# Layer 2's routing stage: weights and head constants loaded from another point, constant rows by DMA from stored patterns, VectorE's additions between pieces of other jobs

## The chip, the core and the metric

One core of one Trainium2 chip runs the whole program. The metric is the device time of one execution in microseconds (us). The kernel before took 1200.81 us, the median of 3 runs (1198.93 to 1203.05).

## What is computed

Two layers on x of 4 x 512 tokens of width 256. Each layer is x + attention(LN(x)) + FFN(LN(x)), cut here to what matters:

```python
xn = _layernorm(x)                    # layer 1: selective scan + mixture of 16 experts, 4 a token
x = x + _L0_attn_ref(xn, ...) + _L0_ffn_ref(xn, ...)
xn = _layernorm(x)                    # layer 2: chunked scan (SSD) with 64 heads + 16 experts, 2 a token
x = x + _L1_attn_ref(xn, ...) + _L1_ffn_ref(xn, ...)
# _L1_ffn_ref: scores = sigmoid(xn @ gate_w.T); top 2, normalised; dw = their weights
#   y = mlp(xn, sw1, sw2, sw3) + sum over experts of mlp(xn, w1[e], w2[e], w3[e]) * dw[:, e]
# _L1_attn_ref: dt = softplus(proj + bias); A = -exp(A_log); c = cumsum(dt * A) in each chunk
#   Lmat = exp(c[t] - c[s]) for s <= t; states and outputs from Lmat, then gate, norm, projection
```

## The kernel before

Five instruction streams (TensorE `pe`, ScalarE `act`, VectorE `v`, GpSimd `pool`, SyncE `sp`) run in program order and meet at semaphores; the order in each is written out by hand. Layer 1 fills the first half of the execution. Then, for layer 2:

- **Scan out and layer norm.** SP reloads the sums in 8 DMAs of 512 KB (`sums0_load`, L1204), two for each batch of four row tiles. TensorE adds them to the scan's rows (`scan_out_tensor`, L1215 and L1217; tile t = 4b waits for batch b), VectorE adds to x. GpSimd's last accumulating DMA of layer 1 is L1156. After the layer norm TensorE transposes the rows into `xnT` (L226), and SP stores them to `xn_d` (L232).
- **Routing stage** (`phase1_tensor`, `phase1_scalar`, `phase1_vector`). It interleaves three jobs. (1) The shared expert: 12 "up" products n = 0 to 11 (`shared_up_tensor`, L686: eight matmul records, gate then up), each followed by a tanh on ScalarE (L707) and two operations on VectorE (`shared_silu`, L714 and L716); after n = 4, 7, 10 and at the end, four "down" products (`shared_down_tensor`, L698), each added to x by VectorE (`shared_add`, L726). Up product n waits for silu n-2, down product t for addition t-2, since each pair has two banks. (2) Routing: logits (L283), a copy out and transposition back (L320, L292, L327), scores (L335), sigmoid (L342, L344), maxima (L347), their indices (L353, cast in L357), mask (`route_mask_vector`), ranks on TensorE (L299), counts and slots, one-hot rows (L428, L436, L445), token numbers on TensorE (L307) and indices for the gathers (`route_index_vector`, L457 to L460). (3) The scan's step sizes: `dt_tensor` (L1573), `dt_first_scalar`, `dt_log_vector` (L1610 to L1615), `dt_sum_vector` (L1623 to L1630), `dt_parts_vector` (L1637 to L1641), `dt_weights_vector` (L1646). In the VectorE stream `dt_log_vector`, `dt_sum_vector` and `dt_parts_vector` each stand whole ahead of a group of four additions.
- **GpSimd beside it** (`load1_pool`): the shared weights' DMAs (L2284 to L2289), issued once the first row of the layer norm is there, then `dt_weights_pool` and `scan1_constants`: memsets and `affine_select`s over `seg_l` (94 x 1024, bf16) and `crow` (88 x 4096, bf16) (L1507 to L1520). Later it gathers rows for the experts (L1491).
- **SP beside it**: `head_weights` (L1542, L1545) once the first row of the layer norm is there, `layernorm_sync`, `scan1_weights` (L1551 to L1557), `combine_store`, then `heads_out_sync`: three DMAs `cp_d` of the cumulative sums' parts (L1762) when semaphore `dt_dve` has reached `CP_READY`, eight DMAs `dec_d` (L1766), and a wait for all of them (`HEADS_STORED`); behind it `scan1_sync`, with the constants, the first chunk's rows and the weights of the first three experts (L1480, L1481).
- **Scan stage** (`scan1_*`). TensorE starts with `dw_tensor` (L1728, L1734) once all 16 additions are done, then the projections (L1846), the first expert's products (L1417, L1430) between them. ScalarE (L1960) and VectorE wait for `HEADS_STORED` before their first instruction of this stage. TensorE takes expert 0's gate and up product between projections 2 and 3.

Three lines set up waits that the steps touch:

```python
CP_READY order: DT_SUM, CP_READY, DT_W, W_READY = 1, 2, 3, 4   # counts of dt_dve
sp.wait_ge(dt_dve, CP_READY)                                   # heads_out_sync, L1760
act.wait_ge(heads_stored, HEADS_STORED)                        # scan1_scalar
```

Of the kernel before, what the change touches and what calls it, by code (L numbers as in the profile page):

```python
# [28 lines left out]
E = 16  # L29
# [54 lines left out]
def _program(nc, a, out, ctx):  # L84
# [6 lines left out]

    bank = ctx.enter_context(nc.psum_tensor("bank", [P, 8, 512], F32))
# [21 lines left out]
    yo = sb("yo", [P, 5, D])  # L114

# [206 lines left out]
    def route_scores_vector(v, l, nr, m):  # L322
# [6 lines left out]
        if l == 0:  # L329
            vec.done(nc.vector.tensor_reduce(m["mx"], logits[:, :, 0:E], X, ALU.max))  # L330
            v.wait_ge(vec.sem, vec.now)
            nc.vector.tensor_tensor(score, logits[:, :, 0:E], m["mx"].unsqueeze(2).to_broadcast([P, TT, E]),
                                    ALU.subtract).then_inc(s.score_in, 1)
        else:
            nc.vector.tensor_copy(score, logits[:, :, 0:E]).then_inc(s.score_in, 1)  # L335
# [13 lines left out]
    def route_pick_vector(v, l, K, m):  # L349
        top, top_i = m["top"], m["top_i"]  # L350
        v.wait_ge(vec.sem, vec.now)
        for t in range(TT):
            vec.done(nc.vector.max_index(top_i[:, t, :], top[:, t, :], m["score"][:, t, :]))  # L353
# [378 lines left out]
    with ExitStack() as c0:  # L732
# [352 lines left out]
        def layer0_scalar(act):  # L1085
# [9 lines left out]
            act.wait_ge(delta_ready, 4)  # L1095
            gate_tanh(act, 0)
# [137 lines left out]
    HEADS, HD, NS, C1, Q = 64, 8, 128, 768, 64  # L1234
# [7 lines left out]
    with ExitStack() as c1a, ExitStack() as c1:  # L1242
# [76 lines left out]
        w_heads = sem("w_heads")  # L1319

        dt_pe, dt_act, dt_dve = sem("dt_pe"), sem("dt_act"), sem("dt_dve")
        DT_TAKEN, DT_LOG, DT_E, DT_EXP = 2, 3, 4, 5
        DT_SUM, CP_READY, DT_W, W_READY = 1, 2, 3, 4
# [179 lines left out]

        def scan1_constants(pool):
            sel = seg_l[:, :, :, :].rearrange("p s g (h t) -> p (s g) h t", t=Q)
            rows = slice(Q, SEG)
            poo.done(nc.gpsimd.memset(seg_l[:, :, :, :], 0.0))  # L1507
            poo.done(nc.gpsimd.memset(crow[0:Q + 24, :, :, :], 0.0))
            poo.done(nc.gpsimd.memset(xpad[:, :, 0:3], 0.0))
            poo.done(nc.gpsimd.memset(xq[:, :, :, :, :, :], 0.0))  # L1510
            pool.wait_ge(poo.sem, poo.now)
            poo.done(nc.gpsimd.affine_select(out=crow[0:Q, :, :, :], in_=crow[0:Q, :, :, :], compare_op=ALU.is_ge, fill=NEVER,
                                             base=0, pattern=[[0, 2 * HP], [1, Q]], channel_multiplier=-1))
# [34 lines left out]
        def scan1_weights(sp):  # L1548
# [4 lines left out]
            for to, src in ((w_in[:, :, :], a["w_in1"].rearrange("(k p) n -> p k n", p=P)),  # L1553
# [3 lines left out]
                sp.dma_start(to, src).then_inc(w_ssd, 16)  # L1557

        UPS1 = NB * F1
        RANKS1_UP, TOKENS1_UP = 4, 10  # L1560

        def downs1_at(n):

# [84 lines left out]
        def phase1_tensor(pe):  # L1648
# [3 lines left out]
            for n in range(UPS1):  # L1652
# [7 lines left out]
                if n == TOKENS1_UP:  # L1660
                    route_tokens_tensor(pe, 1, K1, m1)
# [747 lines left out]
```

## Time and profile before

| | |
|---|---|
| median of 3 runs | 1200.81 us (1198.93 to 1203.05) |
| profiled execution | 1205.48 us, its span 1203.7 us |
| mean granted TensorE clock | 0.935 |
| busy: TensorE, VectorE, ScalarE, GpSimd | 976.7, 914.1, 497.0, 434.9 us |
| routing stage, from the logits to the last addition | about 604 to 711 us of the span |

Times in the rows are counted from the span's start. A row of the timeline is one group of instructions that ran behind one another; what stands in brackets is how long the engine had been idle and what released it. PE is TensorE, DVE VectorE, ACT ScalarE, POOL GpSimd, SPq SyncE's DMA issues. The granted clock is 1.00 at 2.4 GHz and 0.50 at 1.2 GHz.

### The profile page before, as it was taken

How to read it: one execution, taken by the hardware profiler on the slowest of the kernel's cores; microseconds unless marked ns; L12 is line 12 of the kernel's file. 1: busy time of each engine (PE TensorE's matmuls, PEld its weight loads, DVE VectorE, ACT ScalarE, POOL GpSimd, SP SyncE). 2: the span in 40 equal slices, each digit the busy share in tenths (PEclk: the TensorE clock that was granted, in tenths of full speed). 3: DMA queues.
4: the chain of work that ended last, by engine and by line, in shares of the span. 5: the costliest groups of instructions: out<-in, count | busy, mean ns of one | idle time of the engine just before them, and what ended most of it. 6: DMA issues, size and time to landing. Idle time of an engine off the chain costs nothing. (4 is left out here: it accounts for less than half of the span.)

```text
span 1203.7 us, 18601 instructions
## 1 busy us (share of the span) xinstructions
PE 976.7 (81%) x6048; PEld 578.1 (48%) x6048; DVE 914.1 (76%) x1506; ACT 497.0 (41%) x1130; POOL 434.9 (36%) x332
## 2 busy tenths in 40 slices
PE   3987997788787778773787686889988988899885
PEld 2354555444444444441634353445555555456553
DVE  4659567989999999999657746677677767677676
ACT  2201135554555555543121124545455554554542
POOL 0000100777787877753171010322322232133310
PEclk9989999989999999995798798999998999999998
DMA  6960172787878878878650041443433343244524
GB/s 220 369 172 1 52 164 74 134 155 144 165 148 156 162 149 159 147 141 182 142 148 5 0 99 38 112 95 86 112 87 93 87 106 93 67 95 104 116 40 141
DMA packets 107092, 143.27 MB, mean 119 GB/s; under 512 B 30022, under 2 KB 97334, under 8 KB 102710
## 3 DMA queue, kind: packets, MB, share of 16 engines
q0 software_dynamic: 30368, 77.92, 33.5%
q1 hardware_dynamic: 76630, 64.14, 19.2%
q8 instruction: 52, 0.85, 0.3%
q14 instruction: 42, 0.34, 0.1%
HBM read 72.80 MB, written 39.46 MB: 93 GB/s over the span
## 5 line engine op out<-in xcount | busy, mean ns | idle before, releaser
L1501 POOL DMA_INDIRECT sum<-yo,to_i x48 | 78.0, 1624 | 317.1 <-ACT yo L1459 301.2
L1171 POOL DMA_INDIRECT xg<-xn_d,token_i x80 | 96.2, 1203 | 175.1 <-DVE to_i L460 93.4
L1164 POOL DMA_INDIRECT sum<-yo,to_i x80 | 140.3, 1754 | 46.8 <-DMA sum<-yo,to_i 23.7
L1011 PE MATMUL bank<-areaA,xgT 128*128 x320 | 120.6, 502 | 15.0 <-issue 9.9
L1028 PE MATMUL bank<-areaA,hidT 88*128 x320 | 91.7, 410 | 45.8 <-ACT hidT L1076 41.7
L2048 DVE TENSOR_TENSOR areaD<-areaD,gb 128x512 f32<-128x512 f32 x128 | 87.5, 688 | 53.0 <-ACT areaD L1995 49.2
L1028 PEld LDWEIGHTS bank<-areaA,hidT 88*128 88x128 f32 x320 | 55.6, 193 | 76.7 <-issue 72.1
L686 PE MATMUL bank<-xnT,areaB 128*128 128x512 f32 x192 | 86.8, 599 | 0.8 <-DVE y L716 0.8
L1846 PE MATMUL bank<-xnT,w_in 128*128 128x512 f32 x160 | 85.5, 661 | 2.2 <-ACT ecn L1751 1.5
L1011 PEld LDWEIGHTS bank<-areaA,xgT 128*128 128x128 f32 x320 | 56.8, 196 | 58.0 <-issue 41.5
L1491 POOL DMA_INDIRECT xg<-xn_d,token_i x48 | 53.9, 1123 | 82.6 <-DVE to_i L460 68.2
L1995 ACT ACTIVATE areaD<-bank 128x512 f32<-128x512 f32 x128 | 75.9, 593 | 17.0 <-PE bank L1838 15.8
L1058 ACT ACTIVATE areaB<-delta,a_neg 128x1022 f32<-128x1022 f32 x64 | 72.8, 1137 | 4.2 <-DVE areaB L1145 4.2
L1430 PE MATMUL bank<-wst,xgT 128*128 128x352 f32 x192 | 71.3, 496 | 3.6 <-ACT xgT L1446 3.5
L707 ACT ACTIVATE areaB<-bank 128x512 f32<-128x512 f32 x24 | 14.3, 597 | 122.0 <-PE bank L686 122.0
L1083 ACT ACTIVATE yo<-bank,slot_w 128x256 f32<-128x256 f32 x80 | 37.7, 472 | 59.3 <-PE bank L1028 53.5
L2103 DVE SCALAR_TENSOR_TENSOR cv<-xpad,conv_w,cv 128x512 f32<-128x512 f32 x72 | 54.1, 751 | 8.4 <-ACT cv L1961 6.7
L981 PE MATMUL bank<-parts,pick 96*128 96x512 bf16 x128 | 40.6, 400 | 22.7 <-DVE xnT L1145 11.9
L686 PEld LDWEIGHTS bank<-xnT,areaB 128*128 128x128 f32 x192 | 35.4, 190 | 48.4 <-issue 44.4
L1885 PE MATMUL bank<-areaD,xq 128*32 128x64 f32 x2048 | 56.2, 231 | 2.9 <-DVE areaD L2056 2.9
L698 PE MATMUL bank<-areaB,y 128*128 128x256 f32 x192 | 48.3, 413 | 11.2 <-DVE x L728 11.2
L1885 PEld LDWEIGHTS bank<-areaD,xq 128*32 128x32 f32 x2048 | 35.7, 112 | 44.7 <-issue 34.8
(342 smaller groups left out, 2141.6 us busy)
## 6 DMA issues: line engine op xcount, KB each, us to landing
y<-xnT POOLq DMA_DIRECT2D x21, 1024.0 KB
wst<-gu_f SPq DMA_DIRECT2D x96, 176.0 KB
y<-areaB POOLq DMA_DIRECT2D x11, 1024.0 KB
wst<-down_f SPq DMA_DIRECT2D x48, 176.0 KB
areaA<-in_gu SPq DMA_DIRECT2D x2, 2816.0 KB
gu_f<-in_gu POOLq DMA_DIRECT2D x1, 5632.0 KB, 17.0
sum<-yo SPq DMA_DIRECT2D x2, 2176.0 KB, 16.2
down_f<-in_down POOLq DMA_DIRECT2D x1, 2816.0 KB, 22.6
```

Of the source, the lines that this page charges most:

```text
L686: last = nc.tensor.matmul(bank[:, b, :], w[:, k, f * P:(f + 1) * P], xnT[:, k, c * 512:(c + 1) * 512], start=(k == 0), stop=(k == KD - 1))
L1011: last = nc.tensor.matmul(bank[:, GB + q % 2, 0:2 * FI], xgT[:, q % 2, k, :], wgu0_of(e, k), start=(k == 0), stop=(k == KD - 1))
L1028: last = nc.tensor.matmul(bank[:, HY, 0:D], hidT[:, q % 2, h, :], wd0_of(e, h), start=(h == 0), stop=(h == 1))
L1058: nc.scalar.activation(dA[:, u % 2, :].rearrange("p (b t) -> p b t", b=2)[:, :, 1:L], view[:, :, 1:L], ACT.Exp, scale=a_neg[:, hf, n:n + 1 ...
L1164: nc.gpsimd.indirect_dma_start(sum0_d[q % 2], bass.IndirectOffsetOnAxis(ap=to_i[:, q:q + 1], axis=0), yo[:, q % 5, :], None, compute_op=AL ...
L1171: nc.gpsimd.indirect_dma_start(xg[:, q % 5, :], None, xn_d[0], bass.IndirectOffsetOnAxis(ap=token_i[:, q:q + 1], axis=0)).then_inc(s.gathe ...
L1430: last = nc.tensor.matmul(bank[:, eb, 0:2 * FI], xgT[:, q % 2, k, :], wgu_of(q, k), start=(k == 0), stop=(k == KD - 1))
L1501: nc.gpsimd.indirect_dma_start(sum1_d, bass.IndirectOffsetOnAxis(ap=to_i[:, q:q + 1], axis=0), yo[:, q % 4, :], None, compute_op=ALU.add). ...
L1846: last = nc.tensor.matmul(o, w_in[:, k, col:col + P], xnT[:, k, b * L:(b + 1) * L], start=(k == 0), stop=(k == KD - 1))
L1885: last = nc.tensor.matmul(bank[32 * c:32 * c + 32, YB, at_t:at_t + Q], window, mm[:, g, j * Q:(j + 1) * Q], start=(old % 2 == 0 and g == 0 ...
L1995: nc.scalar.activation(ex[:, g % 2, :], o, ACT.Exp).then_inc(free, 1)
L2048: nc.vector.tensor_tensor(mm[:, g, :].rearrange("p (j t) -> p j t", t=Q), ex[:, g % 2, :].rearrange("p (j t) -> p j t", t=Q), gb[:, step % ...
```

## The change

The order of the streams changes in the routing stage, some work moves to the program's start, and the layer-2 constants come by DMA:

- `patterns_pool` builds one 94 x 640 bf16 tile at the program's start; `patterns_store` writes it to HBM (SP, behind the clearing of the sums). `crow_pattern_sync` and `seg_pattern_sync` fill `crow` (704 rows of 1 KB) and `seg_l` (752 rows of 256 B) from it with broadcast reads. The affine_selects over the full tiles go; the memsets of `xpad`, `xq` and `restart` move ahead.
- `load1_pool` waits for the end of layer 1's scan (`hc_ready`) in place of the first row of the layer norm, and `head_weights` for the end of layer 1's experts.
- The scores are copied from PSUM directly (`route_scores1_vector`; the second copy, L335, goes); four of the sixteen `max_index` move one step forward.
- `dt_log_vector`, `dt_sum_vector` and `dt_parts_vector` are cut into pieces, one for each addition of a group; `route_slots_vector` moves from n = 6 to n = 8; the one-hot rows, `dt_weights_vector`, the token rows, the index and the parts move back, so that `CP_READY` is reached at the stage's end. TensorE's token product moves behind down product 12.

```diff
@@ route_scores1_vector (new), route_find_vector (new, cut out of route_pick_vector)
+    def route_scores1_vector(v, m):
...
+        nc.vector.tensor_copy(m["score"].rearrange("p (c j) n -> p c j n", j=4), by_token[:, :, :, 0:E]).then_inc(s.logits, 1)
+        v.wait_ge(s.logits, LOGITS_READ)
+        v.sem_inc(s.score_in, 1)
@@ layer0_scalar
             act.wait_ge(delta_ready, 4)
+            act.wait_ge(pattern_stored, 16)
@@ order of dt_dve
-        DT_SUM, CP_READY, DT_W, W_READY = 1, 2, 3, 4
+        DT_SUM, DT_W, CP_READY, W_READY = 1, 2, 3, 4
@@ patterns
+        def patterns_pool(pool):
...
+            poo.done(nc.gpsimd.memset(pat, 0.0))
...
+            pool.sem_inc(patterns, 1)
+        def patterns_store(sp):
+            sp.wait_ge(patterns, 1)
+            sp.dma_start(pat_d, pat).then_inc(pattern_stored, 16)
+        def crow_pattern_sync(sp):
+            sp.wait_ge(pattern_stored, 16)
+            sp.wait_ge(ly[0].y_ready, NT0)
+            sp.dma_start(crow[0:Q + 24, :, :, :].rearrange("p s (g j) t -> p (s g) (j t)", j=8),
+                         pat_d[0:Q + 24, P:].unsqueeze(1).to_broadcast([Q + 24, 2 * G1, 8 * Q])).then_inc(pattern_rows, 16)
+        def seg_pattern_sync(sp):
+            sp.wait_ge(q1.xn_rows, TT)
+            sp.dma_start(seg_l[:, :, :, :].rearrange("p s g x -> p (s g) x"),
+                         pat_d[:, 0:P].unsqueeze(1).to_broadcast([SEG, 2 * G1, P])).then_inc(pattern_rows, 16)
         def scan1_constants(pool):
+            pool.wait_ge(ly[0].y_ready, NT0)
             poo.done(nc.gpsimd.memset(xpad[:, :, 0:3], 0.0))
             poo.done(nc.gpsimd.memset(xq[:, :, :, :, :, :], 0.0))
+            pool.wait_ge(q1.xn_rows, 1)
             poo.done(nc.gpsimd.memset(restart[:, :], 1.0))
...
         def head_weights(sp):
-            sp.wait_ge(q1.xn_rows, 1)
+            sp.wait_ge(ly[0].y_ready, NT0)
         def scan1_weights(sp):
+            seg_pattern_sync(sp)
@@ phase1_tensor
-                if n == TOKENS1_UP:
-                    route_tokens_tensor(pe, 1, K1, m1)
...
                 shared_down_tensor(pe, 1, F1, sd1, shT1, NB - 1, j)
+                if j == 0:
+                    route_tokens_tensor(pe, 1, K1, m1)
@@ phase1_vector
+                if n == 4:
+                    for j in range(4):
+                        dt_log_vector(v, j)
+                        shared_add(v, 1, None, 0, j)
...
+                if n == 7:
+                    for j in range(4):
+                        dt_sum_vector(v, j)
+                        shared_add(v, 1, None, 1, j)
+                if n == 8:
                     route_slots_vector(v, 1, K1, m1)
                 if n == 9:
+                    route_rows_vector(v, 1, K1, m1, 0, 2 * part)
+                    dt_weights_vector(v)
                 if n == 10:
                     for j in range(4):
+                        if j < 2:
+                            route_rows_vector(v, 1, K1, m1, (2 + j) * part, (3 + j) * part)
+                        else:
+                            route_tile_rows_vector(v, 1, K1, m1, (j - 2) * 2 * part, (j - 1) * 2 * part)
+                        shared_add(v, 1, None, 2, j)
+            route_token_rows_vector(v, 1, K1, m1, 0, TT)
             for j in range(4):
                 shared_add(v, 1, None, NB - 1, j)
+                if j == 1:
+                    route_index_vector(v, 1, m1)
+                dt_parts_vector(v, j)
@@ scan1_sync: the wait for the constants
-            sp.wait_ge(consts1, 2)
+            sp.wait_ge(pattern_rows, 16 * 2)
@@ load1_pool
-            pool.wait_ge(q1.xn_rows, 1)
+            pool.wait_ge(hc_ready, UN)
@@ the streams
             clear_sums(sp)
+            patterns_store(sp)
...
             head_weights(sp)
+            crow_pattern_sync(sp)
             layernorm_sync(sp, 1, xn_tok1)
...
             constants(pool)
+            patterns_pool(pool)
```

## Rows read from the trace of the kernel before

**Rows 1.** Windows: engines' busy us (instructions), granted TensorE clock, DMA share, GB/s.

```profile
660.00:680.00 20.00, 11.82 (x30) 7.08 (x29) 11.36 (x24) 2.32 (x3) 0.00 (x0) 0.74 0.00 0
...
800.00:1100.00 300.00, 273.80 (x2587) 163.51 (x2576) 216.18 (x425) 151.52 (x359) 86.38 (x63) 0.97 0.39 91
```

**Rows 2.** Waits, 600 to 712 us: us in total, times, longest.

```profile
PE bank L698 <- DVE x L726: 8.9, 3, 8.2
```

**Rows 3.** Timeline of VectorE, five short operations of the same engine.

```profile
616.85 2.59 DVE L335 COPY area<-area 128x256 f32<-128x256 f32 x1
...
620.67 4.06 DVE L342 TENSOR_SCALAR area<-area 128x256 f32<-128x256 f32 x1
...
631.80 3.55 DVE L357 CAST area<-area 128x32 f32<-128x32 uint32 x1
...
661.88 0.18 DVE L416 CAST area<-area 128x32 int32<-128x32 f32 x1
...
711.56 1.13 DVE L2018 TENSOR_SCALAR w_out<-w_out,norm_w 128x256 f32<-128x256 f32 x4
```

**Rows 4.** Timeline of GpSimd beside them.

```profile
615.23 4.07 POOL L1512 TENSOR_SCALAR_AFFINE_SELECT crow<-crow 64x4096 bf16<-64x4096 bf16 x1 [0.15 <-POOL xq L1510]
...
620.51 4.08 POOL L1518 TENSOR_SCALAR_AFFINE_SELECT crow<-crow 24x4096 bf16<-24x4096 bf16 x1
```

**Rows 5.** Timeline of TensorE in the routing stage and after it.

```profile
608.94 3.67 PE L686 MATMUL bank<-xnT,sg 128*128 128x512 f32 x4 [3.40 <-DMA sd<-in_sdown]
...
668.85 1.65 PE L698 MATMUL bank<-sd,area 128*128 128x256 f32 x3 [8.18 <-DVE x L726]
...
698.17 1.88 PE L686 MATMUL bank<-xnT,sg 128*128 128x512 f32 x4
...
703.90 7.13 PE L698 MATMUL bank<-sd,area 128*128 128x256 f32 x24 [2.13 <-DVE area L716]
711.55 1.97 PE L1728 MATMUL bank<-ident,areaD 128*128 128x128 f32 x16 [0.52 <-DVE x L726]
...
721.35 1.35 PE L1430 MATMUL bank<-wst,xgT 128*128 128x352 f32 x4
```

**Rows 6.** Timeline of VectorE: a job ahead of additions, and the last addition.

```profile
640.00 1.22 DVE L1610 SCALAR_TENSOR_TENSOR areaD<-areaD 128x1024 f32<-128x1024 f32 x1
...
644.45 0.74 DVE L726 TENSOR_TENSOR x<-bank,x 128x256 f32<-128x256 f32 x2
...
651.88 0.69 DVE L714 SCALAR_TENSOR_TENSOR th<-th,bank 128x512 f32<-128x512 f32 x1 [3.64 <-ACT th L707]
...
663.89 0.87 DVE L1623 TENSOR_SCALAR areaD<-areaD,a 128x512 f32<-128x512 f32 x2
...
679.63 4.42 DVE L428 TENSOR_TENSOR area<-area,iota 128x4096 f16<-128x4096 f32 x1
...
711.07 0.42 DVE L726 TENSOR_TENSOR x<-bank,x 128x256 f32<-128x256 f32 x1 [0.87 <-PE bank L698]
```

**Rows 7.** Timeline of SyncE's DMA issues at the stage's end.

```profile
695.17 1.75 SPq L1762 DMA_DIRECT2D cp_d<-areaD  x3
696.97 5.19 SPq L1766 DMA_DIRECT2D dec_d<-areaD  x8
711.59 0.34 SPq L1776 DMA_DIRECT2D dec<-dec_d  x1
...
715.42 0.94 SPq L1480 DMA_DIRECT2D wst<-gu_f  x2
```

**Rows 8.** Timeline of ScalarE, its first instruction of the scan's loop.

```profile
717.97 0.60 ACT L1960 ACTIVATE xpad<-bank 128x512 f32<-128x512 f32 x1 [2.22 <-PE bank L1846]
```

**Rows 9.** Timeline of TensorE: row tile 12 of the scan out.

```profile
586.20 0.60 PE L1215 MATMUL bank<-areaA,ident 128*128 128x256 f32 x2
```

**Rows 10.** DMA queues, 580 to 585 us (first) and 605 to 610 us: packets, MB, share.

```profile
q1 hardware_dynamic: 1185, 1.16, 66.2%
...
q0 software_dynamic: 319, 0.32, 30.5%
```

More of the change, by code:

```diff
@@ L347, in route_top_vector, with route_find_vector, route_pick_vector @@
             vec.done(nc.vector.max(m["top"][:, t, :], score[:, t, :]))
-    def route_pick_vector(v, l, K, m):
+    def route_find_vector(v, m, t0, t1):
+        v.wait_ge(vec.sem, vec.now)
+        for t in range(t0, t1):
+            vec.done(nc.vector.max_index(m["top_i"][:, t, :], m["top"][:, t, :], m["score"][:, t, :]))
+    def route_pick_vector(v, l, K, m, t0=0):
         top, top_i = m["top"], m["top_i"]
-        v.wait_ge(vec.sem, vec.now)
-        for t in range(TT):
-            vec.done(nc.vector.max_index(top_i[:, t, :], top[:, t, :], m["score"][:, t, :]))
+        route_find_vector(v, m, t0, TT)
         vec.done(nc.vector.tensor_reduce(m["mx"], top[:, :, 0:K], X, ALU.add))
@@ L1517, in scan1_constants @@
-            for part in range(3):
-                poo.done(nc.gpsimd.affine_select(out=by_group, in_=by_group, compare_op=ALU.not_equal, fill=-1.0,
-                                                 base=-part * 8, pattern=[[0, 2 * G1], [-1, 8], [0, Q]], channel_multiplier=1))
-                poo.done(nc.gpsimd.affine_select(out=sel[rows], in_=sel[rows], compare_op=ALU.not_equal, fill=1.0,
-                                                 base=-(24 + 2 * part), pattern=[[0, 2 * G1], [-1, 2], [0, Q]], channel_multiplier=1))
-                pool.wait_ge(poo.sem, poo.now)
@@ L1531, in dt_weights_pool @@
+            pool.sem_inc(consts1, 2)
+        def dt_weights_pool(pool):
             pool.wait_ge(heads_in, 16 * 5)
@@ L1559, in _program @@
         UPS1 = NB * F1
-        RANKS1_UP, TOKENS1_UP = 4, 10
+        RANKS1_UP = 4
         def downs1_at(n):
@@ new lines, in dt_sum_vector @@
+        def dt_sum_vector(v, j):
+            v.wait_ge(vec.sem, vec.now)
+            if j == 0:
+                v.wait_ge(a_ready, 2)
+                for hf in range(2):
+                    vec.done(nc.vector.tensor_scalar(hk(rest1)[:, hf], dtT[:, hf], a1[:, hf:hf + 1], None, ALU.mult))
+            if j in (1, 2):
+                v.wait_ge(consts1, 1)
+                vec.done(nc.vector.tensor_tensor_scan(cT[:, j - 1, :], restart[:, :], rest1[:, j - 1, :], 0.0, ALU.mult, ALU.add))
+            if j == 3:
+                for hf in range(2):
+                    by_chunk = hk(cT)[:, hf]
+                    last = nc.vector.tensor_tensor(l1[:, hf, :, :], by_chunk[:, :, Q - 1:Q].to_broadcast([P, CH, Q]), by_chunk, ALU.subtract)
+                last.then_inc(dt_dve, 1)
@@ L1684, in phase1_vector @@
             route_rows_of_logits_vector(v, 1, m1)
+            part = n1 // 4
             for n in range(UPS1):
```

122 lines of the change are left out of this document (56 added, 66 removed).

## The prediction

> **What bounds the kernel now.** I read the windows first. In the scan stage behind, TensorE is busy 273.8 of 300 us; in the routing stage it has 11.8 of 20 us in one window, at a mean granted clock of 0.74 [rows 1]. The change touches the routing stage, so the question is what holds TensorE there. The waits say: VectorE's additions, 8.9 us in three waits [rows 2]. The timeline shows the pattern. A whole job of VectorE stands ahead of four additions (640.00 to 644.45, then the additions), down products 2 and 3 can't start, and then VectorE waits 3.64 us for up product 5 [rows 6]. The longest such hole on TensorE is 8.18 us, and the work behind it is slow [rows 5]. Second, three short operations of VectorE take 2.59, 4.06 and 3.55 us, where one like the second takes 0.28 (1.13 for four) and a cast of the same size as the third 0.18 [rows 3]. Each ends about when a 4.1 us affine_select of GpSimd over `crow` does: the first at 619.4 with the one that began at 615.23; there are four of these [rows 4]. Third, up product 0 waits 3.40 us for its weights, and its first half takes 3.67 us instead of 1.88 [rows 5]. The stage ends for TensorE with the last addition, 711.07 + 0.42 = 711.5 [rows 6].
>
> **The change, part by part.** I walked the three streams in order, each instruction starting when its engine is free and what it waits for is there: up product 3.43 us (two halves 1.72 apart, 1.88 the last shown) [rows 5], silu 1.33, addition 0.37, down product 1.28 us, everything at 2.4 GHz. The old order gives the last addition at 706.0, where the trace has 711.5; the 5.5 us are spells at 1.2 GHz, as behind the 8.18 us hole. The new order, walked in the same way, gives 687.4, so **18.6 us less** at full clock:
> - Weights earlier: -5.0. The wait (3.4) goes, and with it the slow first half (3.67 - 1.88 = 1.8, less 0.2 of overlap) [rows 5].
> - GpSimd's full tiles go: L335 goes (2.5), L342 becomes 0.3 (-3.8), L357 0.2 (-3.4), 9.7 in all [rows 3]. VectorE then waits 3.7 us for the tanhs (an up product and a `dt` product take 5.3 us a step), so -6.0.
> - dt_log in pieces: -0.3 only. The first addition comes 1.2 us behind silu 4 instead of 4.45, but silu 4 itself is now late: `dt_first_scalar` holds ScalarE for 5.8 us, which VectorE's slowness hid before.
> - Slots moved, dt_sum in pieces: -6.2. Between silu 6 and the first addition stood 2.4 + 2.9 + 1.3 + 4.5 = 11.1 us, now 2.4 + 1.3 + 0.95 = 4.7. The job begins at 663.89 before [rows 6].
> - Rows and parts: -5.0. From silu 8's end to the first addition were 4.3 [rows 6] + 1.3 + 3.8 + 1.3 + 4.6 = 15.3 us, now 2.9 + 1.3 + 3.4 + 1.3 + 1.1 = 10.0; the pieces give 0.3 back.
> - The tail: +4.0. Token rows (1.9), TensorE's token product (1.35) and the parts' pieces now lie between up product 11 and the last addition.
>
> Clock: the new walk leaves TensorE three idle stretches of 2 to 3 us and one of 1.8. In the trace a stretch of 2.13 us is followed by products that take 7.13 us for 24 records, where 12 take 2.57 at full clock [rows 5], so one such stretch costs about 2 us. Bounds 0 and 8; I take 4, against 5.5 before, so **-1.5**. The Trainium skill speaks against the change here: "TensorE: Matmul & The Clock Gate", section "HAM oscillation", tells of kernels whose short idle gaps send the clock back and forth, each burst starting cold. By that every gap would pay, which I estimate at 8 to 10 us instead of 4 and a total of 1195 instead of 1190.
>
> Transfers: the shared weights (1.1 MB) are now issued at about 571 instead of 595, behind L1156 on GpSimd's queue, while SP's last reloads still run: 1185 packets, 66.2% of 16 engines over 5 us, so 45 ns each [rows 10]. The weights were 960 packets, at 75 ns where nothing held them (319 in 30.5%) [rows 10]. On one engine of 16 the two together need 74 x 0.045 + 60 x 0.075 = 7.8 us instead of 3.3, so the last reload lands 4.5 us later, at about 588.4 instead of 583.9. Row tile 12 wants it at 586.20 [rows 9]: **+2.2** on everything behind. Bounds: 0 (the reload is served first) and 4.5 (no slack at tile 12).
>
> Costed at nothing: the patterns at the start (GpSimd is idle there, SP issues one DMA more ahead of a load with 100 us to spare); the broadcasts into `crow` and `seg_l` on SP (first read in the scan stage; w_heads behind them has some 3 us); `head_weights` on SP earlier; the memsets on GpSimd; the stored rows of the layer norm, which silu 0 waits for and which land about when the first tanh is ready (5 us later costs 0.7 in the walk); the gathers, whose index comes 4 us ahead of the last addition and which TensorE wants 6 us behind it. If the first cover fails the price is under 1 us each.
>
> The export: `CP_READY` moves from 16 us ahead of the last addition (695.17) to 0.7 us behind it. Behind the wait on SP are queued three DMAs (1.8 us of issue), eight DMAs (5.19), their landing, then the constants and the experts' weights [rows 7]. Counting from the last addition: issue ends at 0.75 + 1.8 + 5.2 = 7.75, landed at about 9.4 (1.7 us for a small DMA: no row shows it; at least 1, and 4 if they collide with the gathers). ScalarE, which began its loop at 717.97 - 711.49 = 6.5 [rows 8], is held to 9.4: +2.9. The first expert's weights are issued at 9.4 + (715.42 - 711.59) = 13.2 instead of 3.9 [rows 7] and land some 4 us later, at 17.3, while TensorE took the product at 721.35 - 711.49 = 9.9 [rows 5]: +7.4 for it, and project 3 stands behind it in TensorE's order, at half clock after a 4.7 us hole. ScalarE had some slack on project 3, so the scan begins later by between 2.9 and 9.3; nearest the product's own +7.4, I take **+7.0**. TensorE bounds what follows [rows 1], so none of it comes back.
>
> Sum: -18.6 - 1.5 + 2.2 + 7.0 = **-10.9 us**. The profiled execution took 1205.5 (span 1203.7 + 1.8), 4.7 above the median of the runs; against the median the forecast is 1200.8 - 10.9 = **1190 us**.
>
> **Rivals.**
> 1. *The export costs little.* If ScalarE's slack hides the late weights and only +2.9 is left, the time is 1186; with a clock that stays up, 1182. For it: ScalarE and VectorE, not TensorE, set the pace of the first projections. Chance 0.17.
> 2. *The gain stays, but SP gives it back.* cp_d and dec_d share engines with four gathers that are in flight then; if they land 4 us late and the reload costs 4.5, 1190 + 4 + 2.3 = 1196 to 1199, nearly no change. Chance 0.10.
> 3. *Slower: TensorE's clock.* Place: from down product 2 to the last addition, some 54 us. The pieces cut one long hole into many short ones. If the clock is granted in full in none of them, each 3.4 us at half clock costs 1.7. The gain is gone and the kernel slower by 0.3% from (10.9 + 3.6) / 1.7 = 8.5 such spells beyond the two or three I count, 11 in all, or 38 of the 54 us; fully half clock gives about 1213. For it: a mean of 0.74 in a window of before. Against it: that window had the 8.18 us hole. The Trainium skill's section on oscillation, cited above, is the rule that would bring it about. Chance 0.05.
> 4. *The change doesn't do what it says:* the three slow operations aren't GpSimd's doing. Then about 6 us stay in, and the time is 1196. Against it: all three end with an affine_select [rows 3, 4]. Chance 0.03.
>
> **How the numbers follow.** The forecast has 0.65. Its own bounds (clock -4 to +4, transfers -2.2 to +2.3, export -4.1 to +2.3, partly together) give 1183 to 1197; with most of rivals 1 and 2 the range is 1181 to 1198. About 0.3%, 3.6 us, is what a measurement of this kernel can tell from no change. Faster by more needs a time below 1197.2: all of the forecast but a little, rivals 1 and 4: 0.87. Within 0.3%: most of rival 2 and the forecast's rim, 0.08. Slower: 0.05.
>
> **What would show it.** Right: L342 near 0.3 us, the last addition at 691 to 696, TensorE's waits for additions under 3 us each, row tile 12 waiting 1 to 3 us for a reload, cp_d issued behind the last addition, ScalarE idle to 9 us behind it, the first expert product 15 us or more behind it. Wrong: a last addition later than 700, or a scan stage that starts as soon behind it as before.

## The result, and the profile after

The changed kernel took 1195.82 us (median, 1189.17 to 1200.18 in 14 runs), the kernel before 1202.86 (1198.41 to 1208.05 in 14 runs beside it): **ratio 0.9935, 95% interval 0.9914 to 0.9957**, so 7.8 us less by the ratio (5.2 to 10.3; the two medians differ by 7.0). The forecast was 1190 us and 10.9 us less; the range 1181 to 1198 holds the result. Of the 5.8 us between forecast and result, 2.1 are the kernel before, whose median was 1200.81 in the 3 runs that the forecast started from.

The profiled execution took 1190.80 us, its span is 1189.0, the clock 0.945. Against the span of before it is 14.7 us shorter, more than the runs say. The reason lies upstream: layer 1's scan out began at 568.70 instead of 572.97 us, though of layer 1's streams only ScalarE's has something new in it, one wait for the stored patterns; in the profiles of this study it began anywhere from 568.7 to 576.1. So I compare stretches, each from a fixed event to the next, and not spans.

TensorE's timeline of the changed kernel: row tile 12 of the scan out, the logits and up product 0, the products that wait for an addition, the scan's first transposes, and the first expert product:

```profile
568.70 1.19 PE L1229 MATMUL bank<-areaA,ident 128*128 128x256 f32 x2 [10.95 <-DMA y<-areaB]
...
584.54 0.67 PE L1229 MATMUL bank<-areaA,ident 128*128 128x256 f32 x2 [2.92 <-DMA x<-sum]
...
601.98 1.92 PE L288 MATMUL bank<-xnT,wr 128*32 128x512 f32 x16 [0.74 <-ACT xnT L219]
603.83 1.98 PE L699 MATMUL bank<-xnT,sg 128*128 128x512 f32 x4
...
632.28 2.86 PE L711 MATMUL bank<-sd,area 128*128 128x256 f32 x12 [2.33 <-DVE x L739]
...
649.46 3.01 PE L711 MATMUL bank<-sd,area 128*128 128x256 f32 x12 [1.43 <-DVE x L739]
...
668.40 4.54 PE L711 MATMUL bank<-sd,area 128*128 128x256 f32 x12 [3.04 <-DVE x L739]
...
688.53 3.19 PE L1784 MATMUL bank<-ident,areaD 128*128 128x128 f32 x16 [2.13 <-DVE x L739]
...
709.69 2.71 PE L1446 MATMUL bank<-wst,xgT 128*128 128x352 f32 x4 [2.35 <-DMA wst<-down_f]
```

Against [rows 5]: up product 0 has no wait for weights and a fast first half, and the 8.18 us hole is now at most 3.04 us. Row tile 12, which had no wait [rows 9], now waits 2.92 us for the reload. Twelve down records take 2.86 and 3.01 us behind waits of 2.33 and 1.43, and 4.54 behind the wait of 3.04.

VectorE's timeline, what answers to [rows 3] and [rows 6]:

```profile
613.39 0.29 DVE L352 TENSOR_SCALAR area<-area 128x256 f32<-128x256 f32 x1
...
620.99 0.12 DVE L370 CAST area<-area 128x32 f32<-128x32 uint32 x1
...
629.35 0.69 DVE L727 SCALAR_TENSOR_TENSOR th<-th,bank 128x512 f32<-128x512 f32 x1 [2.78 <-ACT th L720]
...
688.06 0.42 DVE L739 TENSOR_TENSOR x<-bank,x 128x256 f32<-128x256 f32 x1
```

The operations of 4.06 and 3.55 us take 0.29 and 0.12; silu 4 waits for the tanh; the last addition ends at 688.5 instead of 711.5. What happened behind it stands in SyncE's DMA issues and in one row of ScalarE:

```profile
689.15 2.49 SPq L1818 DMA_DIRECT2D cp_d<-areaD  x3
691.68 4.67 SPq L1822 DMA_DIRECT2D dec_d<-areaD  x8
702.08 0.35 SPq L1832 DMA_DIRECT2D dec<-dec_d  x1
...
705.54 0.94 SPq L1496 DMA_DIRECT2D wst<-gu_f  x2
```

```profile
702.24 0.60 ACT L2016 ACTIVATE xpad<-bank 128x512 f32<-128x512 f32 x1 [8.16 <-DMA dec_d<-areaD]
```

Against [rows 7, 8]: the last `dec_d` is issued at 696.35, and the wait for it ends at 702.05. ScalarE begins its loop 13.8 us behind the last addition (6.5 before), the first expert product comes 21.2 us behind it (9.9 before).

### The profile page after: what moved, and what is told of

Its sections match the earlier page's. It is cut to its first block, busy times and chain, and to the rows that moved or that the text cites. A ratio compares the mean times of both kernels' runs of the same rounds, so it can differ in the third digit from the quotient of the medians.

```text
span 1189.0 us, 18608 instructions
## 1 busy us (share of the span) xinstructions
PE 970.0 (82%) x6048; PEld 573.3 (48%) x6048; DVE 902.7 (76%) x1508; ACT 495.4 (42%) x1130; POOL 413.9 (35%) x331
## 3 DMA queue, kind: packets, MB, share of 16 engines
q0 software_dynamic: 30368, 77.92, 33.1%
## 4 chain that ended last, share of the span: by engine, by line
PE 45%; DVE 22%; DMA 10%; issue 8%; ACT 6%; POOL 6%; SPq 2%; ACTq 1%; DVEq 0%; POOLq 0%
PE bank L699 7%; DMA sum<-yo,to_i 6%; PE bank L1902 6%; PE bank L1446 4%; PE bank L711 4%; POOL sum L1178 3%; PE bank L1452 3%; POOL xg L1185 3%; DVE cv L2159 2%; PE bank L1941 2%; PE bank L1024 2%; DVE xnT L1159 2%; PE bank L1885 2%; PE bank L1041 2%; PE bank L1894 2%
## 5 line engine op out<-in xcount | busy, mean ns | idle before, releaser
L1185 POOL DMA_INDIRECT xg<-xn_d,token_i x80 | 95.9, 1198 | 175.7 <-DVE to_i L473 94.0
L1024 PE MATMUL bank<-areaA,xgT 128*128 x320 | 116.2, 486 | 15.6 <-issue 8.7
L1902 PE MATMUL bank<-xnT,w_in 128*128 128x512 f32 x160 | 86.7, 668 | 6.6 <-ACT cv L2017 5.4
L1041 PEld LDWEIGHTS bank<-areaA,hidT 88*128 88x128 f32 x320 | 54.9, 190 | 76.4 <-issue 72.1
L1507 POOL DMA_INDIRECT xg<-xn_d,token_i x48 | 54.4, 1133 | 104.4 <-DVE to_i L473 90.0
L2051 ACT ACTIVATE areaD<-bank 128x512 f32<-128x512 f32 x128 | 75.8, 592 | 16.1 <-PE bank L1894 14.7
L994 PE MATMUL bank<-parts,pick 96*128 96x512 bf16 x128 | 40.6, 400 | 22.4 <-DVE xnT L1159 11.0
L711 PE MATMUL bank<-areaB,y 128*128 128x256 f32 x192 | 48.8, 416 | 11.2 <-DVE x L741 11.2
## 6 DMA issues: line engine op xcount, KB each, us to landing
gu_f<-in_gu POOLq DMA_DIRECT2D x1, 5632.0 KB, 18.5
```

What stands on the lines that cost most here:

```text
L711: last = nc.tensor.matmul(bank[:, 4 + n % 2, 0:D], shT[:, (c * F + f) % shT.shape[1], j * P:(j + 1) * P], sd[:, f, :], start=(f == 0), sto ...
L1024: last = nc.tensor.matmul(bank[:, GB + q % 2, 0:2 * FI], xgT[:, q % 2, k, :], wgu0_of(e, k), start=(k == 0), stop=(k == KD - 1))
L1041: last = nc.tensor.matmul(bank[:, HY, 0:D], hidT[:, q % 2, h, :], wd0_of(e, h), start=(h == 0), stop=(h == 1))
L1185: nc.gpsimd.indirect_dma_start(xg[:, q % 5, :], None, xn_d[0], bass.IndirectOffsetOnAxis(ap=token_i[:, q:q + 1], axis=0)).then_inc(s.gathe ...
L1902: last = nc.tensor.matmul(o, w_in[:, k, col:col + P], xnT[:, k, b * L:(b + 1) * L], start=(k == 0), stop=(k == KD - 1))
```

## The experiments

The table has the same stretches from each of the fourteen profiles, in us. Scan out: from its first row tile to the logits. Then, counted from the logits: the start of silu 4, and the ends of the four groups of additions A to D (D is the last addition). Silu 4 is VectorE's first operation on up product 4. Last two columns: from D to ScalarE's loop and to the first expert product.

| kernel | ratio (95%) | scan out | silu 4 | A | B | C | D | ScalarE | expert |
|---|---|---|---|---|---|---|---|---|---|
| before | 1 | 30.7 | 35.1 | 44.6 | 71.1 | 95.2 | 107.9 | 6.5 | 9.9 |
| after | 0.9935 (0.9914-0.9957) | 33.3 | 27.4 | 34.2 | 51.9 | 71.4 | 86.5 | 13.8 | 21.2 |
| e1 export first | 0.9899 (0.9858-0.9940) | 33.3 | 27.4 | 34.2 | 51.9 | 71.5 | 86.6 | 7.9 | 14.7 |
| e2 weights wait | 0.9912 (0.9881-0.9944) | 29.6 | 27.4 | 35.1 | 53.6 | 73.2 | 88.3 | 15.0 | 22.6 |
| e3 experts early | 0.9837 (0.9805-0.9870) | 32.6 | 27.4 | 34.9 | 53.6 | 73.0 | 88.4 | 7.2 | 10.6 |
| e4 both | 0.9844 (0.9806-0.9881) | 31.2 | 27.4 | 34.2 | 51.9 | 71.5 | 86.5 | 7.6 | 11.0 |
| e5 patterns alone | 1.0036 (1.0005-1.0068) | 30.3 | 38.5 | 49.8 | 76.4 | 100.5 | 113.2 | 6.5 | 9.9 |
| e6 orders alone | 1.0000 (0.9972-1.0028) | 30.0 | 36.5 | 45.6 | 63.4 | 83.0 | 98.1 | 14.2 | 22.4 |
| e7 affines back | 0.9850 (0.9805-0.9894) | 32.7 | 27.4 | 34.2 | 51.9 | 72.4 | 86.7 | 7.2 | 10.4 |
| e8 jobs whole | 0.9992 (0.9960-1.0024) | 34.9 | 27.4 | 39.6 | 63.3 | 87.9 | 102.9 | 7.6 | 10.9 |
| e9 weights alone | 1.0144 (1.0106-1.0182) | 56.6 | 29.6 | 40.7 | 67.0 | 91.1 | 103.8 | 6.5 | 9.9 |
| e10 patterns, weights | 0.9982 (0.9949-1.0016) | 35.5 | 27.4 | 39.6 | 65.3 | 89.4 | 100.4 | 6.5 | 9.9 |
| e11 additions first | 0.9756 (0.9720-0.9792) | 30.2 | 27.4 | 33.0 | 49.7 | 67.5 | 82.0 | 7.3 | 10.7 |
| e12 two first | 0.9765 (0.9725-0.9805) | 31.0 | 27.4 | 33.1 | 49.7 | 68.2 | 83.3 | 7.8 | 11.2 |

### The export and the reload: e1 to e4

**e1**: the changed kernel with the eight `dec_d` DMAs, whose data is long there, ahead of the wait for `CP_READY`.

```diff
+            sp.wait_ge(dt_act, DT_E)
+            for b in range(NB):
...
             sp.wait_ge(dt_dve, CP_READY)
             for r in range(3):
...
-            sp.wait_ge(dt_act, DT_E)
-            for b in range(NB):
...
```

> The changed kernel, with the eight small dec_d DMAs issued ahead of the three cp_d DMAs instead of behind them (they need only ScalarE's exponentials, which are there some 30 us before the last addition). Theory A (the changed kernel loses 7 to 10 us behind its stage because ScalarE waits for dec_d's landing, 13.8 us behind the last addition where it was 6.5 before, and the experts' weights are issued behind that): ScalarE's loop begins 6 to 8 us behind the last addition, the first expert product 14 to 16 us behind it instead of 21.2, and the time falls by 5 to 7 us below the changed kernel, to a ratio of about 0.988 of the kernel before. Rival (the landing is late for the gathers and cp_d that share the DMA engines, so it is cp_d that will be late now): ScalarE still begins 11 us or more behind the last addition, gain under 2 us.

Everything up to D is as in the changed kernel, and ScalarE's loop comes 7.9 us behind D instead of 13.8, released by TensorE and no longer by a DMA:

```profile
699.16 0.60 ACT L2016 ACTIVATE xpad<-bank 128x512 f32<-128x512 f32 x1 [2.22 <-PE bank L1902]
```

The expert product stays late (14.7): its weights are still queued behind `HEADS_STORED`. The profile gives 6 us or more; the ratio by itself (0.9899 against 0.9935, each against its own runs of before) doesn't tell e1 from the changed kernel.

**e2**: the changed kernel, but GpSimd issues the shared weights once the last reload has landed (`pool.wait_ge(x_back[NB - 1], 32)`).

> The changed kernel, with GpSimd waiting for the last reload of layer 1's sums before it issues the shared weights. Theory A (the weights delay the last reload, so that row tile 12 waits 2.9 us): row tile 12 waits for nothing, the stretch from the first row tile to the logits takes 30.6 us as before instead of 33.3, and the weights, issued at about 584, are still there when the logits are done, so 2 to 3 us less than the changed kernel. Rival (the weights, now issued beside the scattered 4-byte loads of the head constants, land after the logits, as in the kernel before): up product 0 waits 1 to 5 us, gain nil or a loss of up to 2 us.

The scan out takes 29.6 us instead of 33.3 and row tile 12 has no wait, so the weights' DMAs are what delayed the reload. In this profile groups A and B come 0.9 and 1.7 us later: the twelve products behind the same wait of 2.33 us took 4.33 us where the changed kernel's took 2.86. So only half of the gain is left at D, and the ratio can't be told from that of the changed kernel. The profiles of the other kernels agree on the cause: with the weights issued at layer 1's end the scan out took 32.6 to 35.5 us (after, e1, e3, e7, e8, e10), with the weights behind the reloads or where they were before, 29.6 to 31.2 (before, e2, e4, e5, e6, e11, e12).

**e3**: as e1, and the weights of the first experts are issued on SP before `cp_d` too.

```diff
+            sp.wait_ge(dt_dve, DT_W)
+            for m in range(-5, 0):
+                expert_sync(sp, m)
             sp.wait_ge(dt_dve, CP_READY)
@@ scan1_sync
-            for m in range(-5, 0):
-                expert_sync(sp, m)
```

> Export first, and also the weights of experts tiles 0 and 1 issued ahead of cp_d, once the expert numbers are there (about 25 us before the last addition). Theory A (behind the export the first expert product still waits for its own weights, and project 3 behind it): the first expert product is taken 9 to 11 us behind the last addition as in the kernel before, TensorE waits for no weights, and 2 to 5 us come off e1's time; ratio to the kernel before 0.983 to 0.988. Rival (VectorE and ScalarE pace the first projections, so that the product is not missed): the time is that of e1 within 1 us.

The first expert product is 10.6 us behind D, near the 9.9 of before, and has no wait for weights. Ratio to before 0.9837 against 0.9935, and the intervals don't meet: the two parts of the export's loss were `dec_d` and the weights behind it.

**e4**: e2 and e3 together.

> e2 and e3 together. If the two losses are separate, as theory A has it, the gains add: 9 to 14 us less than the changed kernel, 17 to 21 less than the kernel before, ratio 0.983 to 0.986. If either turns into a wait elsewhere, it gives no more than the better of the two.

Scan out 31.2, expert product 11.0. The ratio is in the range that I expected but can't be told from e3's, so the runs don't show that the two gains add.

### Where the stage's gain comes from: e5, e6, e9, e10

**e5**: the kernel before with the patterns alone: `patterns_pool`, `patterns_store`, `crow_pattern_sync`, `seg_pattern_sync` and the new `scan1_constants`; waits, weights and orders as before.

> The kernel before with the patterns by DMA and nothing else: the full-tile affine_selects of GpSimd go, the weights, the orders and the second copy of the scores stay. My theory (GpSimd's affine_selects hold VectorE's short operations): the copy, the TENSOR_SCALAR and the cast that took 2.59, 4.06 and 3.55 us take about 0.4, 0.3 and 0.2; the part from the logits to the last addition (107.5 us before) comes to 98 to 102, the export costs nothing (last addition to first product of the scan's experts near 10 us), and the time is 0.4 to 0.8% below before. Rival (they are slow of themselves or by DMA traffic): one or more of the three still takes over 2 us and the ratio is within 0.3% of 1.

Slower, and both theories missed. The three short operations are quick (0.29, 0.28, 0.12 us), as my theory had it, but the stage is 5.3 us longer. TensorE's waits and VectorE's timeline of e5 say why:

```profile
PE bank L702 <- DMA sd<-in_sdown: 8.4, 1, 8.4
```

```profile
621.31 0.69 DVE L730 SCALAR_TENSOR_TENSOR th<-th,bank 128x512 f32<-128x512 f32 x1 [14.78 <-DMA xn_d<-area]
```

```profile
598.45 0.42 SPq L1551 DMA_DIRECT2D crow<-pat_d  x1
601.99 0.38 SPq L237 DMA_DIRECT2D xn_d<-area  x1
602.41 12.71 SPq L1557 DMA_DIRECT2D seg_l<-pat_d  x1
```

The 704 KB broadcast into `crow` goes out 3 us after the first shared weights and just ahead of the layer norm's rows. (`seg_l`'s goes out right behind those rows; the two broadcasts weren't tried apart.) The weights land late (a wait of 8.4 us, 3.4 before), and the rows, which silu 0 waits for, take 19.3 us to land instead of 13.6 (8.5 in the changed kernel, where the broadcast goes out at 577.28).

**e6**: the kernel before with the new orders and pieces alone; affine_selects, late weights and the second copy stay.

> The kernel before with the new order and pieces of VectorE's and TensorE's jobs alone: the affine_selects, the late weights and the second copy stay. My theory: the short operations stay at 2.6 to 4 us, the part from the logits to the last addition is 7 to 12 us shorter than before's 107.5, and nearly all of it is given back behind the last addition, where the first expert product comes about 21 us behind it instead of 10.3: a ratio of 0.997 to 1.003. Rival (the export's loss was that of the weights and not of the order): first expert product within 12 us of the last addition and a ratio under 0.995.

As my theory had it: D comes 9.8 us sooner, the expert product 12.5 us later behind it, and the ratio is 1.0000. ScalarE's row shows the same late landing as in the changed kernel: the last `dec_d` was issued by 708.31, and ScalarE started 6.3 us later.

```profile
714.64 0.60 ACT L1978 ACTIVATE xpad<-bank 128x512 f32<-128x512 f32 x1 [8.58 <-DMA dec_d<-areaD]
```

**e9**: the kernel before with the weights and head constants issued sooner alone (and GpSimd's memset of `restart` held until the layer norm's first row).

```diff
-            pool.wait_ge(q1.xn_rows, 1)
+            pool.wait_ge(hc_ready, UN)
@@ head_weights
-            sp.wait_ge(q1.xn_rows, 1)
+            sp.wait_ge(ly[0].y_ready, NT0)
```

> The kernel before with the shared weights and the head constants issued sooner, and nothing else (GpSimd waits for the layer norm's first row only ahead of its memset of restart). My theory, from the walk's term: up product 0 no longer waits for its weights (3.4 us before) and its first half takes 2 us, so the part from the logits to the last addition comes to 101 to 104 us instead of 107.9; the scan out is 2 to 3 us longer, as in the changed kernel (30.65 to 33.3). Ratio 0.995 to 0.999. Rival (the stage is held by VectorE's short operations behind GpSimd anyway): the stage stays within 1.5 us of 107.9 and the ratio is 1.000 to 1.003.

From the logits to D the number is the one that my theory gave (103.8, 4.0 less than before), but the run doesn't price the weights alone. The full tiles were through before the logits, so the short operations were quick here too:

```profile
640.35 0.28 DVE L342 TENSOR_SCALAR area<-area 128x256 f32<-128x256 f32 x1
...
648.52 0.12 DVE L357 CAST area<-area 128x32 f32<-128x32 uint32 x1
```

And the kernel is 17 us slower by the ratio: the scan out takes 56.6 us instead of 30.7. GpSimd's stream is in order: before, it waited 8.9 us for the head constants and began the full tiles at 609.3; with those constants early the wait is gone, and the full tiles begin at 596.0, in the midst of the layer norm. VectorE's groups by line, 590 to 626 us of e9, then 590 to 604 of before (count, busy us, mean ns), and GpSimd's timeline in e9:

```profile
L202 DVE TENSOR_SCALAR area<-x,ln 128x256 f32<-128x256 f32 x16 | 29.9, 1941 | 0.0
```

```profile
L202 DVE TENSOR_SCALAR area<-x,ln 128x256 f32<-128x256 f32 x16 | 6.3, 466 | 0.0
```

```profile
602.20 4.07 POOL L1512 TENSOR_SCALAR_AFFINE_SELECT crow<-crow 64x4096 bf16<-64x4096 bf16 x1 [0.15 <-POOL xq L1510]
...
618.25 4.08 POOL L1518 TENSOR_SCALAR_AFFINE_SELECT crow<-crow 24x4096 bf16<-24x4096 bf16 x1
622.28 1.20 POOL L1520 TENSOR_SCALAR_AFFINE_SELECT seg_l<-seg_l 30x1024 bf16<-30x1024 bf16 x1
```

Sixteen row operations take 29.9 us instead of 6.3. The expected ratio was wrong, since I had not asked what GpSimd does next. No run has the earlier weights with the full tiles still in the stage; what the weights are worth is read from the timelines further down.

**e10**: e5 with the earlier weights and head constants: both halves of the new loading, all orders as before. The broadcast into `crow`, which stands behind the head constants on SP, goes out sooner with them (578.73 instead of 598.45), so that e10 doesn't say which of the two moves cured e5.

> The patterns alone made the kernel slower (ratio 1.0036): the 704 KB broadcast of crow stood ahead of the shared weights and of the layer norm's stored rows, and up product 0 waited 8.4 us and silu 0 14.8 us. This kernel adds the earlier weights to it and leaves all orders as before. My theory: with the weights out of the way at 576 us, the stored rows land in 8 to 10 us instead of 19.3, neither wait is left, and the part from the logits to the last addition is 97 to 101 us (113.2 with the patterns alone, 107.9 before), the scan out 2 to 3 us longer; ratio 0.993 to 0.997. Rival (the broadcasts themselves hold the rows): silu 0 still waits over 5 us for the stored rows, and the ratio stays at 0.999 or above.

No wait for weights, silu 0 at 6.3 us as in the changed kernel, D at 100.4 instead of 107.9. The scan out is 4.9 us longer, where I had expected 2 to 3, so the ratio, 0.9982, is outside the 0.993 to 0.997 of my theory and is not told from 1: of patterns and early weights each alone costs time (e5, e9), together they give the stage 7.4 us and take some of it back in the reload.

### Alternating, and GpSimd's hold by itself: e8, e7

**e8**: e3 with the jobs at the same places but whole ahead of their group.

```diff
                     for j in range(4):
                         dt_log_vector(v, j)
+                    for j in range(4):
                         shared_add(v, 1, None, 0, j)
```

(and so for `dt_sum_vector` and for the one-hot rows at n = 10)

> The version with export and expert weights ahead of cp_d, with dt_log, dt_sum and the one-hot rows standing whole ahead of their group of four additions again, each at the same place, so that alternating is the only thing undone. My theory: TensorE's waits for the first addition of a group grow by 1 to 3 us each and the stage is 2 to 6 us longer, ratio 0.986 to 0.990 against 0.984. Rival (the hand walk's own figure: alternating brings 0.3 us at the first group, about 2 at the others and nothing at the clock): under 1.5 us and a ratio within 0.1% of 0.984.

Far more than either theory gave: D is 14.6 us later than in e3, and the ratio 0.9992 instead of 0.9837. TensorE's waits of e8, then of e3:

```profile
PE bank L711 <- DVE x L739: 17.3, 3, 6.4
```

```profile
PE bank L711 <- DVE x L739: 6.8, 3, 3.1
```

The waits account for 10.5 us; the rest is the clock. The twelve records behind each of the three waits take 5.49, 5.49 and 5.14 us, 4.6 more in all than in e3 (4.12, 3.01 and 4.42). The three of e8, then the first of e3:

```profile
639.14 5.49 PE L711 MATMUL bank<-sd,area 128*128 128x256 f32 x12 [5.64 <-DVE x L739]
...
662.88 5.49 PE L711 MATMUL bank<-sd,area 128*128 128x256 f32 x12 [5.29 <-DVE x L739]
...
687.77 5.14 PE L711 MATMUL bank<-sd,area 128*128 128x256 f32 x12 [6.37 <-DVE x L739]
```

```profile
636.80 4.12 PE L711 MATMUL bank<-sd,area 128*128 128x256 f32 x12 [2.33 <-DVE x L739]
```

**e7**: e3 with a memset and five affine_selects of 24 x 4096 on GpSimd from the logits on, over a tile that nobody reads then (SP issues the experts' weights, which go into that tile, once the selects are done).

> The version with export and expert weights ahead of cp_d, plus a memset and five affine_selects of 24 x 4096 (about 4.1 us each) on GpSimd from the logits on, over a tile that nobody reads then. It measures the hold by itself. My theory: operations of VectorE that take 0.1 to 0.7 us without them (TENSOR_SCALAR, cast, silus' second half) are stretched to 1 to 4 us, ending when an affine_select ends, and the stage is 2 to 7 us longer, ratio 0.985 to 0.992 against 0.984 without. Rival: no VectorE operation is stretched and the ratio stays at 0.984.

VectorE's and GpSimd's timelines of e7:

```profile
620.21 3.42 DVE L352 TENSOR_SCALAR area<-area 128x256 f32<-128x256 f32 x1
623.66 1.75 DVE L354 RECIPROCAL area<-area 128x256 f32<-128x256 f32 x1
...
630.82 1.13 DVE L370 CAST area<-area 128x32 f32<-128x32 uint32 x1
...
636.17 0.69 DVE L727 SCALAR_TENSOR_TENSOR th<-th,bank 128x512 f32<-128x512 f32 x1 [0.79 <-ACT th L720]
```

```profile
610.97 20.94 POOL L2356 TENSOR_SCALAR_AFFINE_SELECT wst<-wst 24x4096 bf16<-24x4096 bf16 x5 [7.91 <-PE bank L288]
```

Five selects of 4.19 us end at 615.2, 619.3, 623.5, 627.7 and 631.9: the TENSOR_SCALAR ends at 623.63 and the cast at 631.95. The hold is real (3.42 us for 0.29, 1.13 for 0.12), and the reciprocal beside it is not held. But silu 4 begins 27.4 us behind the logits, exactly as without: its wait for the tanh shrank from 2.78 to 0.79 us. The 4.1 us of hold cost nothing in this order; here the rival was right on the time, and I on the mechanism.

### A version that beats both: e11, e12

**e11**: e4, with each addition of groups A to C ahead of its piece.

```diff
                     for j in range(4):
-                        dt_log_vector(v, j)
                         shared_add(v, 1, None, 0, j)
+                        dt_log_vector(v, j)
```

> The version with export, experts' weights and the shared weights behind the reloads, plus one thing: in the three groups of four, each addition stands ahead of its piece instead of behind it. My theory: TensorE's waits for the first addition of a group (2.3, 1.4 and 3.1 us) shrink by the length of the first piece (1.2, 0.8, 1.2), and the clock behind them falls less: stage 1 to 5 us shorter than that version's 86.4, ratio 0.980 to 0.984. Rival: the third and fourth additions wait for their products anyway, so the waits only move from the first to the second pair: under 1 us.

```profile
PE bank L711 <- DVE x L739: 3.8, 3, 1.9
```

The waits fall from 6.8 to 3.8 us, D from 86.5 to 82.0. **Ratio 0.9756**: 2.4% less than before and 1.8% less than the changed kernel. The profiles account for 4.5 us of its step beyond e4. The ratios say 0.0088, or 10.6 us, but each is against its own runs of before and known to 0.004, so that the step may be anything from about 4 to 17 us.

**e12**: additions 0 and 1 both ahead of the first piece.

> As the kernel with each addition ahead of its piece, but additions 0 and 1 both ahead of the first piece. TensorE's first two products of a group are long done by then, so products 2 and 3 can run behind one another while VectorE works on pieces 0 and 1. My theory: another 0 to 2 us off the stage against additions first, ratio 0.978 to 0.984. Rival: no difference from it, since product 3 needs the banks only 1.3 us after product 2.

The waits are the same 3.8 us and the ratio 0.9765: no difference, as its rival had it. D comes 1.3 us later in this profile for another reason: behind the same wait of 1.92 us the twelve products of group C took 3.03 us in e11 (first row) and 4.54 here (second):

```profile
664.09 3.03 PE L711 MATMUL bank<-sd,area 128*128 128x256 f32 x12 [1.92 <-DVE x L739]
```

```profile
664.27 4.54 PE L711 MATMUL bank<-sd,area 128*128 128x256 f32 x12 [1.92 <-DVE x L739]
```

## Why the prediction was right, and where it was not

The terms of the sum against what the profiles measured. The stretches are those of the table, from before to after.

| term | predicted | measured |
|---|---|---|
| weights, full tiles: up to silu 4 | -11.0 | -7.7 |
| dt_log in pieces: silu 4 to A | -0.3 | -2.8 |
| slots moved, dt_sum in pieces: A to B | -6.2 | -8.8 |
| rows and parts: B to C | -5.0 | -4.6 |
| tail: C to D | +4.0 | +2.4 |
| clock | -1.5 | (in the rows above) |
| reload | +2.2 | +2.6 |
| export | +7.0 | +9.8 |
| **sum** | **-10.9** | **-9.0** |

(The predicted terms down to the tail add up to -18.5; the walk's total was -18.6.) The export's measured value is the start of TensorE's first product on `xC,xB`, behind the projections, which came 44.6 us behind D before (first row) and 54.4 after (second):

```profile
756.09 0.33 PE L1863 MATMUL bank<-xC,xB 128*128 128x64 f32 x2
```

```profile
742.83 0.33 PE L1919 MATMUL bank<-xC,xB 128*128 128x64 f32 x2
```

The sum of -9.0 lies inside the interval of the runs, -5.2 to -10.3; the forecast's -10.9 is just outside it.

**The stage** (-20.1 against -21.4) came out as walked in total, and nearly all of the signs named ahead were there: the last addition at 688.5, which is 692.8 with layer 1's earlier end (4.3 us) added back; row tile 12 waiting 2.92 us; waits for additions of 2.33 and 1.43 us, and one of 3.04 where all were to be under 3. ScalarE, which was to be idle to 9 us behind the last addition, was idle to 13.8. That the total fits is in part luck, for two errors cancelled in it:

- "GpSimd's full tiles go: -6.0" was too large, and "dt_log in pieces: -0.3 only" too small. The weights gave what was forecast: up product 0 starts 1.9 us behind the logits instead of 5.3, and its first half takes 1.98 us instead of 3.67, so that its second half comes 5.1 us sooner, for the forecast 5.0. Of the 7.7 us up to silu 4 that leaves 2.6 for the full tiles. e10, with the loading but no new order, gains 7.7 us at silu 4 and keeps only 5.0 at A (44.6 to 39.6): with the job whole, TensorE meets a hole of 5.65 us and a slow clock there that the slow VectorE had hidden before, when the mask came late anyway (TensorE waited 5.5 us for it). The pieces then give 5.4 (39.6 to 34.2), and e8 against e3 gives 4.7. A step's worth depends on what stands beside it; I had put the reduced hole down to the removal and left nothing for the alternation.
- Alternating is the main part of the change, once the loading is right: e8 says 14.6 us in three groups. (With the full tiles and the late weights still there, all the new orders together brought D only 9.8 us forward, e6.) I had put the gain of group B on the moved slots; before to e8 that move gives 2.7 us of A to B (26.4 to 23.7), the pieces 5.1 more (23.7 to 18.7).

**The export is the step that failed**, in size. "Issue ends at 7.75" was right (696.35 - 688.48 = 7.87). "Landed at about 9.4 (1.7 us for a small DMA)" was not: the wait ended at 13.6, 5.7 us behind the last issue. So ScalarE was held by 7.3 us instead of 2.9, the weights were issued at 17.1 instead of 13.2, and the product was 11.4 us late instead of 7.4. I had kept 4 as the upper end, for a collision with the gathers. e1 and e3 show the mechanism: with `dec_d` ahead of the wait ScalarE's delay goes, with the weights ahead too, the product's.

**The reload** was right: 2.6 for 2.2, and e2 shows the cause. The size has its scatter: the six kernels with the weights at layer 1's end have a scan out 1.9 to 4.9 us longer than before's.

**"Costed at nothing: the patterns"** holds only in company. e5 shows that the stage is 5 us longer with the broadcasts where the weights go out beside them; e9 that earlier weights cost 17 us with the full tiles still on GpSimd. Neither dependence was in my text.

**The rivals.** Rival 1 needed a cheap export: it was dearer. Rival 2 (SP gives the gain back) is the direction in which the truth lay, by 1.9 us of the sum, and half of its condition came true: `dec_d` landed 4.2 us later than forecast, but the reload cost 2.6 and not 4.5. Its reason, the gathers on the same engines, is not what the trace shows (the last section). For rival 3, the clock: the windows of after give a granted clock of 1.00 from 620 to 660 us and 0.89 from 660 to 680, where before had 0.74 [rows 1]:

```profile
660.00:680.00 20.00, 14.83 (x43) 9.38 (x42) 15.21 (x23) 1.19 (x2) 0.00 (x0) 0.89 0.00 0
```

What the waits for additions did to the twelve products behind them depends on their length, and not on it alone. Behind 1.4 us they took 3.0 us in all seven profiles with such a wait; behind 2.33 us 2.86 in after, e1 and e4, but 4.33 in e2 and 4.12 in e3; behind 1.92 us 3.03 in e11 and 4.54 in e12; behind 3.0 us always 4.4 or more. The Trainium skill's section on oscillation ("TensorE: Matmul & The Clock Gate", "HAM oscillation") tells of a kernel that waits for a DMA between its bursts of products and starts every burst cold; I had read it as every gap paying. The traces agree for the waits of 3 us, in part for those of 1.9 and 2.3, and not for those of 1.4. Rival 4 fell: with the full tiles gone the operations are short (e5), with them back they are long (e7).

## What to carry to other kernels

When one engine works for two, alternate: put the operation that the other engine waits for first and the piece of the unrelated job behind it, since a whole job ahead of it costs its length and then the clock (14.6 us for three groups here, in e8 against e3, and 4.5 more for the order inside a pair, in e11 against e4). Before a wait is moved later, look at what is queued behind it on that engine, above all exports whose data was ready long ago, and take them out from behind it (1.0% here). And an edit that is free in company can cost more than the whole gain alone: moving a stream's first instructions moves all that follows them (e9).

## What the hardware showed that I had not expected

- **Scattered writes land late.** `dec_d` (eight DMAs of 1 KB, in single elements) took 6.1 us from issue to landing by the DMA view of after, against 3.8 for 256 KB of `cp_d`. The packets had ended long before: the windows (the last two columns are DMA share and GB/s) show the DMA engines almost at rest from 698 us on, 4 us ahead of the release at 702.05. In e6, too, the wait ended 6.2 us behind the last issue.

```profile
696.00:698.00 2.00, 2.00 (x7) 0.79 (x5) 0.00 (x0) 0.00 (x0) 0.00 (x0) 1.00 0.25 1
698.00:700.00 2.00, 0.12 (x1) 0.00 (x0) 0.00 (x0) 0.00 (x0) 0.00 (x0) 1.00 0.02 4
700.00:702.00 2.00, 0.00 (x0) 0.00 (x0) 0.00 (x0) 0.00 (x0) 0.00 (x0) 1.00 0.00 0
```

  In e1, where the three `cp_d` are the last in front of the same wait, the engines are busy until shortly before its end at 698.45:

```profile
697.00:698.00 1.00, 0.92 (x2) 0.49 (x3) 0.00 (x0) 0.00 (x0) 0.00 (x0) 1.00 0.56 167
698.00:698.40 0.40, 0.40 (x2) 0.19 (x1) 0.00 (x0) 0.00 (x0) 0.00 (x0) 1.00 0.03 5
```

  The Trainium skill ("DMA: Bandwidth & Descriptors", "Anatomy of one DMA", which is about DMAs that GpSimd issues) puts most of a DMA's fixed cost of about 2 us on the receipt of its last write. For `dec_d`, which SP issues, the trace agrees that the time lies behind the last packets, and has about twice that figure; for `cp_d` in e1 it has under 1 us. That it is the single elements which make the difference is argued from these two and wasn't tried by itself.
- **A DMA's issue can hold its engine for long.** One `seg_l` DMA kept SP for 12.7 us in e5, and one `dt_b` DMA of 0.2 KB kept it for 9.7 us in the changed kernel (600.97 to 610.68), both behind the issue of the layer norm's rows (2 MB), the second also behind that of `seg_l`. In the changed kernel nothing urgent stood behind it.

```profile
600.97 9.71 SPq L1592 DMA_DIRECT2D dt_b<-dt_b_d  x1
```

- **The hold between GpSimd and VectorE** stops copies, casts and TENSOR_SCALARs from SBUF to SBUF until the affine_select ends (the copy of 2.59 us in [rows 3], the cast and the TENSOR_SCALAR in e7), and no reciprocal, maximum or operation with one source in PSUM (e7: 1.75 us for the reciprocal, with and without). The Trainium skill ("SBUF — State Buffer", "SBUF: two separate sides") describes an exclusive lock on a port pair that whoever starts first keeps for its whole instruction; the ends at 623.63 and 631.95 agree with it. e9 shows how dear it can be: 23.6 us over 16 operations, beside GpSimd's work on the full tiles.
